# A two-layer graph network on one core: the end of the attention layer moved beside its gather, gating in rank order, expert results scattered to the output

## The reference, cut to what matters

```python
x = x + gcn(_layernorm(x))                 # gather of rows, normalised sum per destination
x = x + top2_experts(_layernorm(x))        # 8 experts, 256 wide
# attention layer
h = (xn @ W).reshape(n, 4, 64)             # xn = _layernorm(x)
e = leaky_relu(al_src[src] + al_dst[dst], 0.2)
alpha = softmax of e over the edges of each dst
y = segment_sum(h[src] * alpha, dst) + bias_gat + xn @ W_res + b_res
x = x + gamma * (y - mean) * rsqrt(var + eps) + beta
# top-1 experts with a capacity of C = 977 tokens each
probs = softmax(xn2 @ gate_w + gate_b)     # xn2 = _layernorm(x)
idx = argmax(probs); pos = place of the token among those of its expert, in order of node
ybuf = relu(buf @ w1 + b1) @ w2 + b2       # buf[e, pos] = xn2, 1024 wide inside
x = x + nan_to_num(ybuf[idx, min(pos, C-1)] * (prb * (pos < C)))
```

## Time and profile before

| what | us |
|---|---|
| median of 3 runs | 5689.02 (5685.35 to 5697.13) |
| the profiled execution, its own time | 5690.28 |
| its span, first to last instruction | 5688.4 |
| second gather ends on VectorE, `route_phase` begins | 4670.8 |
| gating of all tokens begins | 5034.0 |
| scatter to `sent` | 5052.4 to 5115.4 |
| expert stage | 5121.1 to 5617 |
| `combine_phase`, GpSimd's first DMA | 5618.3 |

### The profile page before, as it was taken

The page is one execution under the profiler, slowest core; times in us unless marked ns, Lnnn a source line. Parts: engine busy times, 40 slices in busy tenths (PEclk is TensorE's granted clock), DMA queues, the critical chain, the costliest instruction groups (busy, mean ns, idle before and its releaser), DMA issues. The chain is left out here.

```text
span 5688.4 us, 78645 instructions
## 1 busy us (share of the span) xinstructions
PE 3682.4 (65%) x19749; PEld 2798.7 (49%) x19749; DVE 3429.4 (60%) x8878; ACT 1182.6 (21%) x3413; POOL 3455.1 (61%) x3590
## 2 busy tenths in 40 slices
PE   6067777777777777756666666666666650048994
PEld 4045666556666666634444444444444430035663
DVE  6455555555555555547777777777777775723343
ACT  4323333333333333410000000000000000022210
POOL 4177777777777777657777777777777740030003
PEclk9589999999999899977777777777777775559997
DMA  4476665556656656534444444444444432112213
GB/s 120 151 220 170 171 170 168 169 169 172 169 170 169 171 169 169 144 107 133 134 133 133 133 134 133 133 132 134 132 132 133 134 98 80 42 36 91 81 63 101
DMA packets 347742, 768.37 MB, mean 135 GB/s; under 512 B 79180, under 2 KB 189730, under 8 KB 347254
## 3 DMA queue, kind: packets, MB, share of 16 engines
q0 software_dynamic: 199216, 583.73, 36.9%
q1 hardware_dynamic: 148166, 180.65, 10.0%
HBM read 704.72 MB, written 60.80 MB: 135 GB/s over the span
## 5 line engine op out<-in xcount | busy, mean ns | idle before, releaser
L813 POOL DMA_INDIRECT flow_rows<-table,edges x1708 | 1623.4, 950 | 641.0 <-issue 498.1
L1360 POOL DMA_INDIRECT gat_steps_rows<-table,edges x1712 | 1662.5, 971 | 559.2 <-issue 498.1
L1164 PE MATMUL flow_sum_ps<-flow_rows,flow_onehot 128*128 128x256 bf16 x5124 | 763.7, 290 | 510.8 <-DMA flow_rows<-table,edges 419.2
L1660 PE MATMUL gat_steps_sum_ps<-gat_steps_rows,gat_steps_onehot 128*128 128x264 f32 x3424 | 1052.3, 465 | 4.5 <-DVE gat_steps_rows L1472 3.5
L1164 PEld LDWEIGHTS flow_sum_ps<-flow_rows,flow_onehot 128*128 128x128 bf16 x5124 | 494.8, 104 | 712.1 <-issue 346.4
L1660 PEld LDWEIGHTS gat_steps_sum_ps<-gat_steps_rows,gat_steps_onehot 128*128 128x128 f32 x3424 | 754.1, 230 | 172.0 <-DVE gat_steps_rows L1472 18.3
L892 DVE TENSOR_TENSOR acc<-flow_sum_ps,acc 128x256 f32 x854 | 360.4, 422 | 675.0 <-PE flow_sum_ps L1164 658.3
L1608 PE MATMUL gat_steps_lanes_ps<-ident,gat_steps_score 128*64 128x128 f32 x214 | 73.6, 448 | 667.8 <-ACT gat_steps_score L1557 667.8
L1472 DVE TENSOR_TENSOR gat_steps_rows<-gat_steps_rows,gat_steps_weight_ps 128x1024 f32<-128x1024 f32 x428 | 505.3, 1200 | 0.2 <-issue 0.2
L1216 PE MATMUL flow_y_ps<-flow_w,flow_hid 128*128 128x256 f32 x1568 | 428.5, 398 | 67.6 <-DVE flow_x_blk L978 44.7
L1206 PE MATMUL flow_hid_ps<-flow_xn_t,flow_w 128*128 128x128 f32 x3136 | 458.1, 294 | 11.7 <-ACT flow_hid L1099 11.7
(11 more groups left out here) (375 smaller groups left out, 5057.5 us busy)
## 6 DMA issues: line engine op xcount, KB each, us to landing
gat_steps_drow<-drow SPq DMA_DIRECT2D x107, 512.0 KB
gat_steps_rows<-table,edges POOLq DMA_INDIRECT x1712
flow_rows<-table,edges POOLq DMA_INDIRECT x1708
expert_w<-in_L_ffn_w SPq DMA_DIRECT2D x16, 1024.0 KB, 9.7
table<-start_parts SPq DMA_DIRECT2D x49, 192.0 KB, 1.9
sent<-flow_zeros SPq DMA_DIRECT2D x8, 1040.0 KB, 18.1
expert_xe<-sent SPq DMA_DIRECT2D x8, 1040.0 KB, 5.7
answers<-expert_y SPq DMA_DIRECT2D x64, 128.0 KB, 1.7
```

Of the source, the lines that this page charges most:

```text
L813: nc.gpsimd.indirect_dma_start(out=rows[n % RING][:, t, :], out_offset=None, in_=g["table0"][:, :], in_offset=bass.IndirectOffsetOnAxis(ap ...
L1164: ins = t.matmul(sum_ps[i % 2][:, :], onehot[i // AHEAD % 2][:, i % AHEAD * T + u, :], rows[i % RING][:, u, part * D:(part + 1) * D], star ...
L1360: nc.gpsimd.indirect_dma_start(out=rows[w % RING][:, t, 0:RW], out_offset=None, in_=g["table1"][:, :], in_offset=bass.IndirectOffsetOnAxis ...
L1660: ins = t.matmul(sum_ps[s % BANKS][:, :], onehot[k][:, i, :], rows[r][:, i, :], start=(i == s * T), stop=(i == s * T + T - 1))
```

## The change

- In `flow_phase` VectorE adds `L1_gnn_beta` to the block of x before it is stored as `x_mid` (one instruction more for each of the 49 blocks, `residual`), and SyncE stores `x_mid` after its wait for `res_ready`.
- `gat_steps_phase` carries what `route_phase` did for each block. A block k begins in the window in which its last sum is added (`begins`), and takes nine stages, three for each window (`tick`): maxima, shares, blend and statistics, scale, join with `x_mid` and statistics, scale, turn, gate, keep. SyncE fetches the block's rows one block ahead, and stores the new x to `x_end`. The norms run on ScalarE. The lists of VectorE, ScalarE and TensorE are written out for all 107 windows instead of looped over. `BANKS` is 3.
- `gates_phase` has what is left of `route_phase`: the gating of all tokens, now in rank order, with the counts before a block made by a matmul over blocks that stand earlier, and each token's name (its node plus one) written beside it.
- `expert_phase` copies `x_end` to the output at its start, memory to memory, between the loads of experts 0 and 1. GpSimd gathers the x rows of a tile's tokens, VectorE adds them (after one more `drain`), and GpSimd scatters the tile to the output. There are four buffers of `y` instead of two. `combine_phase` is gone.

```diff
@@ flow_phase, SyncE store and VectorE residual
-                sp.wait_ge(y_added, b * NY + NY)
-                sp.dma_start(g["x_mid"][bass.ds(at, P), :], x_blk[k][:, :]).then_inc(x_out[k % 2], 16)
                 sp.wait_ge(rows_ready, b + 1)
...
                 sp.wait_ge(res_ready, b + 1)
+                sp.dma_start(g["x_mid"][bass.ds(at, P), :], x_blk[k][:, :]).then_inc(x_out[k % 2], 16)
...
+                dve.wait_ge(xn2_ready, n + 1)
+                ch.link(v.tensor_tensor(xb, xb, next_beta[:, :], ALU.add))
@@ gat_steps_phase
-        BANKS = 4
-        UNROLL = 6
+        BANKS = 3
+        TICKS = 3
+        STAGES = 9
+        def done_by(k):
+            return -(-STEPS * (k + 1) // NB)
+        def begins(k):
+            return (done_by(k) - 1) // SPW * TICKS + TICKS - 1
+        def due(tick):
+            return [(k, tick - begins(k)) for k in range(NB) if 0 <= tick - begins(k) < STAGES]
@@ SyncE
+            def fetch(k):
+                at = row_of(nc, sp, g, k)
+                at_least(sp, var_ready[1], k)
+                for into, arr in ((self_row, "table1"), (res, "residual"), (x_mid, "x_mid")):
+                    sp.dma_start(into[:, :], g[arr][bass.ds(at, P), :]).then_inc(fetched, 16)
+            def store(k):
+                at = row_of(nc, sp, g, k)
+                sp.wait_ge(var_ready[1], k + 1)
+                sp.dma_start(g["x_end"][bass.ds(at, P), :], x_new[:, :]).then_inc(stored, 16)
@@ VectorE
+            def maxima(k):
+                at_least(dve, added, done_by(k))
+                ch.link(v.tensor_tensor(far[0][:, :], acc[:, k, RW:RA], state[:, k, 0, :], ALU.add))
...
+            def shares(k):
+                dve.wait_ge(share_exp, k + 1)
...
+            def blend(k):
+                dve.wait_ge(shared, k + 1)
+                ch.link(v.tensor_tensor(node[:, :], others[:, :], mine[:, :], ALU.add))
+                ch.link(v.tensor_tensor(node[:, :], node[:, :], res[:, :], ALU.add))
+                norm_stats(0, node[:, :])
+            def scales(n, k):
+                dve.wait_ge(root_ready[n], k + 1)
...
+            def join(k):
+                dve.wait_ge(normed[0], k + 1)
+                at_least(dve, stored, 16 * k)
+                ch.link(v.tensor_tensor(node[:, :], node[:, :], gamma[:, :], ALU.mult))
+                ch.link(v.tensor_tensor(x_new[:, :], node[:, :], x_mid[:, :], ALU.add))
+                norm_stats(1, x_new[:, :])
+            def keep(k):
+                dve.wait_ge(logits_ready, k + 1)
+                v.tensor_tensor(g["logit"][:, k, :], logit_ps[:, :], gate_b[:, :], ALU.add).then_inc(logits_kept, 1)
...
                 weigh(w, rw, 0)
                 weigh(w, rw, 1)
+                tick(w * TICKS)
...
                 adds(1)
+                tick(w * TICKS + 1)
...
                 adds(2)
                 adds(3)
+                tick(w * TICKS + 2)
@@ ScalarE
+            def slot(w, more):
+                if more:
+                    scores(n, k, r, n // RING + 1)
+                tick(w * TICKS)
+                tick(w * TICKS + 1)
+                if more:
+                    exps(n, k, r)
...
+                    fades(n, k)
+                tick(w * TICKS + 2)
@@ expert_phase
-                    sp.wait_ge(down_ready, (e - 1) * NT)
+                    sp.wait_ge(y_ready, (e - 1) * NT)
...
             load(0, 0, False)
+            sp.dma_start(out[:, :], g["x_end"][0:NODES, :]).then_inc(filled, 16)
             load(1, 1, False)
...
+                for t in range(NT):
+                    pool.wait_ge(y_ready, e * NT + (t + 1))
+                    nc.gpsimd.indirect_dma_start(
+                        out=out[:, :], in_=y[t % R][:, :], in_offset=None,
+                        out_offset=bass.IndirectOffsetOnAxis(ap=ids[k][:, t:t + 1], axis=0),
+                        bounds_check=NODES - 1, oob_is_err=False).then_inc(y_out[t % R], 16)
...
+                    dve.drain()
+                    dve.wait_ge(x_row_in[t % R], e * (16 * NT // R) + (t // R) * 16 + 16)
+                    v.tensor_tensor(y_, y_, x_row[t % R][:, :], ALU.add).then_inc(y_ready, 1)
```

More of the change, by code:

```diff
@@ new lines, in tick @@
+            def tick(at):
+                for k, stage in due(at):
+                    if stage == 0:
+                        maxima(k)
+                    if stage == 1:
+                        shares(k)
+                    if stage == 2:
+                        blend(k)
+                    if stage == 3:
+                        scales(0, k)
+                    if stage == 4:
+                        join(k)
+                    if stage == 5:
+                        scales(1, k)
+                    if stage == 8:
+                        keep(k)
```

647 lines of the change are left out of this document (268 added, 379 removed).

## The result

The changed kernel takes **5264.4 us**, median of 4 runs (5262.26 to 5274.48), against 5688.29 of the kernel before in the same comparison: a ratio of 0.9257, interval 0.9243 to 0.9271. Five more runs of it in another session gave 5265.22 (ratio 0.9261, 0.9248 to 0.9274). Where the two differ I give both.

A forecast was written before the change was run, and what follows sets the result against it. GpSimd, issuing DMAs without waiting, was taken to bound both gathers, at 20.41 us a window in the second. The sum was 5690.3 - 363.2 + 0.5 + 32 + 17.3 - 66 + 0.5 = 5311 us; range 5270 to 5430.

The forecast's parts named there:

- Terms 1 and 6: Behind the second gather: `route_phase` alone goes, -363.2 us; last windows' stages and block 48's lone chain add 17.3.
- Term 2: Second gather: the stages add 5.8 us of VectorE work a block, 2.66 us a window.
- term 4: Second gather's window ends: late handoffs cost VectorE 0.7 us a window, making it level with GpSimd; surcharge +32 us.
- term 3: Second gather: VectorE's own list is 17.05 us a window, 19.7 with the stages, under GpSimd's 20.41.
- rival D: Second gather: GpSimd stays the only bound and the handoffs hide; 5279 us, chance 0.1.
- Term 7: Experts: tile scatters replace `combine_phase`, only the last expert shows VectorE's lag; -66 us.
- Term 8: Copy of `x_end` before expert 1's loads: no delay taken, 0 us, bounds 0 and +36.
- Term 9: First gather: the added VectorE step and later `x_mid` store cost 0, or 23 without room; start +0.5 us.
- A: Second gather: VectorE is the bound and waits for handoffs; gather grows by 139 us, total 5418, chance 0.14.
- B: Second gather: written-out lists stall on their code, 1.2 us a window, 128 us; total 5407, chance 0.07.
- F: Block stages come late and run behind the gather, 563 us instead of 363; total 5824, chance 0.03 shared with E.
- The lock: Second gather: two-operand VectorE steps lock out GpSimd, 147 us instead of 32; total 5426, chance 0.07.

The follow-up runs named there:

- a4: Changed kernel without the block stages' work on VectorE, ScalarE and TensorE in the second gather, transfers kept: 5256.15 us, one run.
- b2: Kernel before with the second gather's lists for VectorE, ScalarE and TensorE written out for all windows: 5683.8 us, ratio 0.9994.
- d2: Changed kernel, three banks, with an idle VectorE copy of about 0.6 us added in each window: 5335.43 us, ratio 0.9374.
- d1: Changed kernel with four banks for sums instead of three: 5270.39 us, ratio 0.927.
- a1: Changed kernel run again without an edit, in another session: 5265.22 us, ratio 0.9261; its profiled execution took 5261.89.
- d4: Changed kernel with all block stages started after all sums are added, one block after another: 5870.23 us, one run.
- h1: Changed kernel with four banks and the destination one-hot cut into four steps of 512 columns: 5248.58 us, ratio 0.9223.
- g1: Kernel before with the destination one-hot cut into four steps of 512 columns: 5659.69 us, ratio 0.995.
- e1: Kernel before with the one-hot cut into four steps of 512, on a slower chip: 6731.64 us, ratio 1.0076.
- e2: Changed kernel with the one-hot cut into four steps of 512, on a slower chip: 6469.59 us, ratio 0.9689.
- f2: Changed kernel with the one-hot cut into four steps of 512, on a slower chip: 6381.21 us, ratio 0.9509.

## Why the prediction was wrong, point by point

**Terms 1 and 6** (the stage that goes, and the tail): -344.4 against -345.9. From the last DMA to the end of block 48's maxima it took 39.5 us, where 4670.8 - 4637.4 + 5.8 = 39.2 were forecast. The lone chain behind the maxima took 4671.13 to 4683.13 = 12.0 us for 11.5: the load of the exponential's table (1.28) is not hidden when nothing lies beside it and costs 0.5, the norms take 0.60 where I had 0.5, and other parts came out shorter. The turn to the gating's stage took 0.7, which the sum left out. The gating saved 2.4 where I added 0.5.

**Term 2 and the lateness of term 4** were right in size: 2.66 + 0.7 = 3.4 us a window were forecast, 3.3 measured (a4 against after). The base of term 3 was 0.4 too high: I took only the loop's turn of 0.47 off, while b2 gained 0.8 of wait in a window 0.1 shorter. So VectorE's list is 19.9, not 20.4.

**The step that failed is in term 4: "two engines that are level lose something: for that I take 0.3 ... +0.3 x 107 = +32".** With the list at 19.9 and three buffers of rows, GpSimd had no gap over 0.32 us between two DMAs, its gaps added up to the same 521 us as in before, and the surcharge was 0. It showed where VectorE's list is the longer one: d2, at 20.55, ran at 20.77 a window. Without this term the sum is rival D's 5279.

**Behind it stands a second one: GpSimd's 20.41 us a window was taken as fixed,** so 5279 was in effect a floor and the range could not reach far below. The 20.41 held some 0.4 us a window of DMAs lengthened by VectorE's steps (45.5 us in all), and how many steps meet a DMA depends on the phase. In the changed kernel the sum is 32.2 and 27.5: 7 to 11 ns less a DMA over all 1712, which is the 12 to 18 us. Which part of the change moved the phase is open: the written-out lists alone have 35.1 (b2), with three banks but no stages it is 39.3 (a4), with the stages and four banks 39.4 (d1), so no part does it by itself, and that it came out as a gain is luck of the phase. I saw the 1.38 in the earlier trace rows and counted only that new steps could add; a gain was excluded without a reason. From 5279 the rest is small. Measured less forecast, in a1: +2.3 at the start, -18.2 in the gather, +0.8 in the tail, -2.9 in the gating, -0.2 before expert 1, +0.9 in the last stage, 5261.7 in all for 5261.89. In the profile of after: +5.6, -11.9, +1.5, -2.9, +2.1, +0.8, 5274.2 for 5274.48. Besides, the sum started from a profiled execution 2 us above its median.

The start's +2.8 to +6.1 is real, and no experiment explains it. The first DMA of the second gather starts at 2450.8 to 2454.7 in the five profiles of before and its variants (mean 2453.0), and at 2454.7 to 2463.0 in the ten of the changed kernel and its variants (mean 2458.0). Some 5 us belong to the change, 3.5 of them between the first gather's first and last DMA.

**Term 7**: -65.2 against -66. **Term 8**: 0 was right: expert 1's matmuls follow without a wait. **Term 9** put the first gather at 0, with 0.5 for the start; the profiles say some 5 us together, as above. No run tells the added step on VectorE from the later store of `x_mid`.

**The rivals.** A (handoffs waited for) did not come: VectorE was not the bound. B was excluded by b2. C didn't come. D was right in its mechanism (GpSimd the only bound) and 15 us high for the reason above. E didn't come. F is what d4 is, at 5870 instead of 5824.

**The lock.** The prediction gave 0.07 to a total of 5426, in which each two-operand step of a block holds GpSimd up. The timeline of after shows such a step (L1624, both operands in SBUF) beside a DMA of the usual 0.95, and the bf16 one-hot beside one of 1.14; the last two lines are h1's, where the same step (L1626 there) stands beside one of 1.06:

```profile
3017.74 0.95 POOL L1430 DMA_INDIRECT gat_steps_rows<-table,edges  x1 [0.30 <-issue]
3017.83 0.42 DVE L1624 TENSOR_TENSOR gat_steps_x_new<-gat_steps_node,gat_steps_x_mid 128x256 f32<-128x256 f32 x1
...
3032.34 0.75 DVE L1488 TENSOR_SCALAR gat_steps_onehot_t<-gat_steps_drow,pidx 128x2048 bf16<-128x2048 bf16 x1 [0.31 <-issue]
3032.78 1.14 POOL L1430 DMA_INDIRECT gat_steps_rows<-table,edges  x1 [0.30 <-issue]
```
```profile
3007.02 1.06 POOL L1430 DMA_INDIRECT gat_steps_rows<-table,edges  x1 [0.30 <-issue]
3007.30 0.43 DVE L1626 TENSOR_TENSOR gat_steps_x_new<-gat_steps_node,gat_steps_x_mid 128x256 f32<-128x256 f32 x1
```

The 46 DMAs that met this step from 2600 to 4600 us took 0.98 on average in after, up to 1.20, and 1.05 in h1, up to 1.17: over 0.945 that is 1.6 and 5 us in all. Other steps stand close to it there, and no run takes it alone.

The Trainium skill, SBUF — State Buffer, section "SBUF: two separate sides", calls it an exclusive lock held for a whole instruction, and no division of bandwidth. By that a shorter instruction holds it for less, and cutting the one-hot should help although the columns are the same: g1 agrees, with 28 us. For steps with two f32 operands in SBUF the section speaks of a GpSimd operation that reads SBUF, and I priced the issue of a DMA as one. That reading fails by its size: 147 us were to come, a few are there, and the gather became shorter.

## What to carry to other kernels

When one engine issues DMAs back to back and another computes beside it, look at the spread of the DMA's duration, not only at its mean and its waits: what exceeds the minimum is a reserve that a shorter VectorE step can free (here four steps of 512 columns for one of 2048: 28 us of 5688), and that any shift may give or take (25 us by an idle copy, nothing by two). Here it freed time only where that engine sets the pace; on the two other chips the same cut cost 0.8 to 0.9%. Here the second engine could be filled to within 2% of the one that sets the pace without a loss, with three buffers between them; past it a small lag hides in the buffers and shows behind the loop, so read the time from the last issue to the last use. Before adding work to an engine near that edge give it slack on the other side (a fourth bank), and change both together.

## What the hardware showed that I had not expected

- An added 0.6 us of idle work in each of 107 windows made the kernel before 25 us faster (5660.65 against 5685.82), and twice that took the gain back (5688.68 against 5687.63). Both fit one sum: 17.6 and 45.9 us of DMA time over 0.945 us.
- A software DMA of 0.945 us took up to 1.47 beside a bf16 step of 0.75 us, up to 1.20 beside its halves and up to 1.08 beside its quarters. Runs of small steps on VectorE lengthened one to 1.20.
- On two chips the kernel before was 17 and 18% slower (6672.78 and 6712.66), and the changed kernel with the cut one-hot 23 and 21% (6469.59 and 6381.21 against 5271.71), at the same median DMA on GpSimd (0.946 to 0.949 us). The share of the 16 engines that the gathers' queue took was 36.9% of 5688.4 us in before and 31.6% of 6737.6 in e1, 2099 and 2129 us: the packets took hardly longer. GpSimd and VectorE waited for something that the profile calls remote, up to 2.8 us at the DMAs and 8.4 at the adds. The mean granted clock was 0.76 there and 0.81 on the others; whether that is cause or effect, and what the remote waits are, stays open.

```profile
DVE acc L1489 <- remote: 268.8, 54, 8.4
```

- The change is worth 7.4% on the one kind of chip and 3.1 to 4.9% on the other (with the cut one-hot, e2 and f2), where GpSimd does not set the pace in the second gather.
